# Vision tower with experts: first group's factor products in high and low parts, and a new order of units

## The chip, the cores and the metric

The kernel runs on one core of a Trainium2 chip. The metric is the device time of one execution in microseconds. Before the change the median of three runs is 160.95 us (160.54 to 161.43).

## The reference

32 images of 3 x 96 x 96 become patches of 16 x 16 (36 per image), are projected to 256 features, get a class token (37 tokens per image, 1184 in all) and position terms. Then one block follows: attention of a factored form with running sums instead of softmax, and a layer of 8 experts with two choices per token.

```
h = tok(x)                                        # projection, class token, positions
x1 = layernorm(h)
Q, K = x1 @ Wq.T, x1 @ Wk.T;  Z = cumsum(x1) / counts      # along the 37 tokens
bil = ((Q @ V_b) * cumsum(K @ W_b)) @ U_b.T
tri = ((Q @ V_t) * (Z @ X_t) * cumsum(K @ W_t)) @ U_t.T
h = h + ((bil + alpha * tri) / counts + bias) @ Wo.T
x2 = layernorm(h)
gates = softmax(x2 @ w_router + b_router);  top 2; capacity 185 tokens per expert, in token order
y = weighted sum over the kept choices of (gelu(x2 @ w1[e] + b1[e]) @ w2[e] + b2[e])
out = h + y
```

The order of tokens matters twice: the running sums go along an image, and a token's place with an expert is the count of earlier tokens that chose it.

## The kernel before, in words

Features lie on partitions where products are taken (`h_t`, `xn_t`), tokens on partitions where rows are normalised (`xn`, `h2`). The 1184 tokens are ten tiles of 128, in four groups, GROUPS (L26): A tiles 0 to 2, B_ 3 to 5, C 6 and 7, E 8 and 9 (E has 160 tokens, since the last tile holds 32). In the texts a unit is written zc(A), norm2(C) and so on.

The front part of the kernel is a pipeline over groups, written out by hand in four lists. UNITS (L281) is TensorE's order; each unit is a kind, a group and one of four pairs of PSUM banks (the third number). Before a unit is written, `claim` (L1133) makes TensorE wait until the unit that had this pair before has been read by its last reader. The kinds:
- proj: patches times the projection; B_ and C in high and low parts (SPLIT). On VectorE `proj` adds the position terms into `h_t`.
- norm1: transposes of `h_t`; VectorE takes the statistics (`stats1`, `rstd1`), ScalarE the root (`root1`) and the normalised rows (`norm1`).
- xn_t: transposes of these rows back; ScalarE copies them to `xn_t` (`xn_copy`). For a group in PARTED (L37) ScalarE rounds them to float32r (`xn_high`) and VectorE takes the rest (`xn_low`).
- zc and a: the factor products, `factor_product` (L1121). zc holds the two factors whose results go into running sums, a the third. A group outside PARTED uses two float32 products per factor (one for each half of the features); a group in PARTED uses six of float32r: high x high, low x high, high x low. The factors' parts `m_h` and `m_l` are made on ScalarE (`m_high`) and GpSimd.
- VectorE's `sums` are the scans, GpSimd multiplies the scaled sums into `prod`, VectorE's `prod` multiplies by a. y is the output product, `add_up` adds it to `h_t` giving `h2_t`.
- norm2: transposes of `h2_t` with the router products; ScalarE reads the means (`means2`), sums the squares (`squares2`), takes the root (`root2`), copies the rows kept for the output (`keep2`) and writes the normalised rows (`rows2`) after VectorE's reciprocal and logits (`rstd2`).
- slots and pick: the choices are made in two parts (CHOICES, L30: tiles 0 to 5 and 6 to 9). VectorE's `choose` finds the two experts of each token, slots counts on TensorE who came earlier, VectorE's `place` writes one-hot rows for expert 0, `count` reads all places, and pick multiplies the rows by the one-hots, giving the input of expert 0. Tile 5 of the first part is held back to the second pick (HELD).

BRIDGES (L28) puts products with no use ahead of a unit as filler: four ahead of slots(0), three ahead of pick(0), each two records. They stand behind the unit's `claim`. DVE_ORDER (L291) and ACT_ORDER (L296) are the orders of VectorE and ScalarE, POOL_ORDER that of GpSimd's products. SP's queue stores rows in the order in which rows2 and keep2 stand in ACT_ORDER; GpSimd's gathers for experts 1 and 2 wait for these stores and for the looked-up rows `src_row`.

Then come eight experts: up product, gelu, down product (from expert 1 on in high and low parts, with `hid_hl` for the hidden rows), turned out, weighted and added to the output by indirect DMA.

Of the kernel before, what the change touches and what calls it, by code (L numbers as in the profile page):

```python
# [11 lines left out]
KD = D // 128  # L12
# [15 lines left out]
BRIDGES = {('slots', 0): 4, ('pick', 0): 3}  # L28
# [8 lines left out]
PARTED = (1,)  # L37
INSIDE = KP // 2 - 1
GROUP = max(n for _, n in GROUPS) * TT
EVEN = max(GROUPS[g][1] for g in PARTED) * TT  # L40
# [57 lines left out]
def vit_block(nc, first, patches, const, vectors, attn, w1, w2, b2_rows, xrows, out):  # L98
# [6 lines left out]
    with ExitStack() as ctx:  # L105
# [22 lines left out]
        def spread(per_choice, tiles, n, p=TT):  # L128
# [25 lines left out]
        xn_h, xn_l = (t[:, :, :].rearrange("p k n -> p (k n)")[:, 0:KD * EVEN].rearrange("p (k n) -> p k n", k=KD)  # L154
                      for t in (patch_h, patch_l))
# [12 lines left out]
        hid_hl = sb("hid_hl", [128, KF, 2, SL], f32r)  # L168
        out_t, out_low = held(KF + 2 * KD, KD), held(KF + 3 * KD, KD)
# [61 lines left out]
        def bank(b):  # L231
# [50 lines left out]
                 ("norm1", B_, 2), ("xn_t", A, 0), ("proj", E, 3), ("norm1", C, 1), ("xn_t", B_, 0), ("zc", A, 2),  # L282
                 ("zc", B_, 3), ("a", A, 0), ("a", B_, 1), ("norm1", E, 2), ("xn_t", C, 3), ("y", A, 0), ("zc", C, 3),
                 ("y", B_, 1), ("xn_t", E, 2), ("norm2", A, 0), ("zc", E, 3), ("norm2", B_, 2), ("a", E, 1), ("a", C, 3),
                 ("y", E, 1), ("y", C, 3), ("norm2", E, 0), ("slots", 0, 1), ("norm2", C, 2), ("pick", 0, 3),
                 ("slots", 1, 1), ("pick", 1, 3)]
        PLACE = {(kind, n): u for u, (kind, n) in enumerate(unit[:2] for unit in UNITS if unit[0] != "pick")}
        PICK_SLOT = 3


        DVE_ORDER = [("proj", A), ("uw", 0), ("proj", B_), ("proj", C), ("stats1", B_), ("rstd1", B_), ("proj", E),  # L291
                     ("stats1", C), ("xn_low", B_), ("rstd1", C), ("sums", A), ("sums", B_), ("prod", A), ("stats1", E),
                     ("prod", B_), ("rstd1", E), ("add_up", A), ("sums", C), ("add_up", B_), ("sums", E), ("rstd2", A),
                     ("prod", E), ("prod", C), ("rstd2", B_), ("add_up", E), ("choose", 0), ("add_up", C), ("place", 0),
                     ("count", 0), ("rstd2", E), ("rstd2", C), ("choose", 1), ("below", 0), ("place", 1), ("count", 1)]
        ACT_ORDER = [("mac", 0), ("root1", A), ("norm1", A), ("m_high", 0), ("xn_copy", A), ("root1", B_), ("norm1", B_),  # L296
# [791 lines left out]
        def _(pe):  # L1088
# [32 lines left out]
            def factor_product(dst, n, m, factor):  # L1121

                products = [(factor, xn_t[n % 2])]
                if n in PARTED:
                    products = [(m_h[:, m], xn_h), (m_l[:, m], xn_h), (m_h[:, m], xn_l)]
# [302 lines left out]
```

## Time and profile before

| | us |
|---|---|
| median of three runs | 160.95 |
| lowest and highest | 160.54, 161.43 |
| the profiled execution | 159.94 |
| its span, first to last instruction | 158.1 |
| TensorE, VectorE, ScalarE, GpSimd busy in it | 149.5, 103.4, 82.1, 50.8 |

The profile is of one execution. Its page gives busy time by engine, 40 slices of the span, and the chain of work that ended last. A group of instructions is shown with the line that issued it, the tile that it writes and the ones it reads, and how often. On TensorE a float32 product has two records. Ends of matmuls are modelled and overlap the next start by some 0.17 us, so rates are taken from start to start. In this program's lines, L1129 are the factor products, L1162 and L1236 the transposes, L1250 the output product, L1117 the pick, L1146 the filler, L1299 the first up products of expert 0.

### The profile page before, as it was taken

Reading aid. Unit: us, or ns where it says so; the run is one execution under the profiler, and the core shown is the slowest. Engines: PE = TensorE matmul, PEld = TensorE weight load, DVE = VectorE, ACT = ScalarE, POOL = GpSimd, SP = SyncE. Lnnn points to the kernel's source line nnn. Section 1 sums busy time; section 2 is a strip of 40 time slices with the busy share of each in tenths; the row PEclk is TensorE's granted clock in tenths of the full one; section 3 lists DMA queues with packets and bytes.
Section 4 is the critical chain, followed back from the end, with each engine's and each line's share of the span. In section 5 each row is a group of like instructions: output and inputs, shape, how many; then the busy total and the mean of one; then the engine's idle time right before and its main releaser. Section 6 shows DMA issues by size and latency. Waiting matters only on the chain.

```text
span 158.1 us, 3015 instructions
## 1 busy us (share of the span) xinstructions
PE 149.5 (95%) x1010; PEld 139.4 (88%) x1010; DVE 103.4 (65%) x331; ACT 82.1 (52%) x210; POOL 50.8 (32%) x55
## 2 busy tenths in 40 slices
PE   7999999999999889999999999999999999999950
PEld 7559999978788788899799899999999999999950
DVE  0076874579766988981396859669486795794710
ACT  4215544640528989657055657474582665737100
POOL 6003005007230000004537158085372661604351
PEclk9999999999999999999999999999999999999999
DMA  5999960079002273100489887788868988600421
GB/s 173 420 427 406 405 221 0 0 252 326 8 0 92 100 249 130 51 0 26 106 335 298 269 265 185 266 202 300 280 117 281 264 249 255 139 8 0 52 25 23
DMA packets 17123, 28.48 MB, mean 180 GB/s; under 512 B 1149, under 2 KB 13607, under 8 KB 16857
## 3 DMA queue, kind: packets, MB, share of 16 engines
q1 hardware_dynamic: 14649, 25.49, 47.0%
q0 software_dynamic: 2464, 2.86, 10.3%
q8 instruction: 6, 0.10, 0.3%
q14 instruction: 4, 0.03, 0.1%
HBM read 24.21 MB, written 4.14 MB: 179 GB/s over the span
## 4 chain that ended last, share of the span: by engine, by line
PE 69%; DMA 9%; DVE 8%; issue 4%; ACT 3%; POOL 2%; POOLq 1%; SPq 1%; DVEq 0%; ACTq 0%
PE ps L1287 18%; PE ps L1322 10%; PE ps L1225 7%; PE ps L1207 6%; PE ps L1129 6%; DMA w_even<-w 5%; PE ps L1324 4%; PE ps L1162 3%; DMA out_rows<-out_s,dst_row 3%; PE ps L1141 2%; POOL out_rows L496 2%; PE ps L1167 2%; PE ps L1299 2%; DMA rows_in<-xrows,src_row 2%; PE ps L1250 2%
## 5 line engine op out<-in xcount | busy, mean ns | idle before, releaser
L496 POOL DMA_INDIRECT out_rows<-out_s,dst_row x16 | 23.8, 1485 | 38.6 <-ACT out_s L681 32.2
L657 ACT ACTIVATE first_t<-ps,b_cur 128x186 f32<-128x186 f32 x64 | 23.0, 413 | 23.7 <-PE ps L1287 22.1
L1322 PE MATMUL ps<-hid_hl,split 128*128 128x372 f32 x96 | 29.1, 370 | 0.0
L1324 PE MATMUL ps<-hid_hl,split 128*128 128x186 f32 x96 | 23.8, 248 | 0.0
L1287 PE MATMUL ps<-first_t,patch_t 128*128 128x186 f32 x128 | 21.7, 322 | 0.1
L975 DVE CAST hid_hl<-first_t 128x372 fp32r<-128x372 f32 x28 | 10.7, 383 | 15.8 <-ACT first_t L657 15.8
L1287 PEld LDWEIGHTS ps<-first_t,patch_t 128*128 128x128 f32 x128 | 20.1, 190 | 0.4 <-issue 0.4
L481 POOL DMA_INDIRECT rows_in<-xrows,src_row x14 | 15.6, 1112 | 12.9 <-DVE src_row L943 9.0
L1287 PE MATMUL ps<-first_t,w_even 128*128 128x186 f32 x112 | 18.9, 321 | 0.0
L1324 PEld LDWEIGHTS ps<-hid_hl,split 128*128 128x128 f32 x96 | 18.3, 191 | 0.0
L521 ACT ACTIVATE split<-patch_t 128x512 fp32r<-128x512 f32 (+2 forms) x28 | 13.7, 552 | 8.8 <-DMA patch_t<-patches 5.1
L1322 PEld LDWEIGHTS ps<-hid_hl,split 128*128 128x128 f32 x96 | 18.0, 188 | 0.0
L1287 PEld LDWEIGHTS ps<-first_t,w_even 128*128 128x128 f32 x112 | 17.6, 190 | 0.0
L977 DVE TENSOR_TENSOR hid_hl<-first_t,hid_hl 128x372 fp32r<-128x372 f32 x28 | 15.3, 547 | 1.0
L564 ACT ACTIVATE xn<-ps,nmr,rstd 128x256 f32<-128x256 f32 (+1 forms) x20 | 9.7, 556 | 2.2 <-DVE nmr L740 2.2
L1207 PE MATMUL ps<-split 128*128 128x360 f32 (+1 forms) x72 | 10.6, 305 | 0.0
L983 DVE TENSOR_TENSOR split<-patch_t,split 128x512 fp32r<-128x512 f32 x16 | 10.2, 684 | 0.0
L1207 PEld LDWEIGHTS ps<-split 128*128 128x128 f32 x72 | 10.2, 188 | 0.0
L521 ACT ACTIVATE first_t<-ps 128x186 f32<-128x186 f32 x13 | 4.2, 322 | 10.7 <-PE ps L1324 9.7
L1225 PE MATMUL ps<-first_t 128*128 128x396 f32 x24 | 8.5, 510 | 0.0
L983 DVE TENSOR_TENSOR split<-w_even,split 128x512 fp32r<-128x512 f32 x12 | 7.7, 685 | 0.9 <-ACT split L521 0.9
L1225 PEld LDWEIGHTS ps<-first_t 128*128 128x128 f32 x24 | 4.5, 197 | 3.5 <-DMA first_t<-first 0.7
(175 smaller groups left out, 268.8 us busy)
## 6 DMA issues: line engine op xcount, KB each, us to landing
w_even<-w SPq DMA_DIRECT2D x8, 1024.0 KB, 5.7
patch_t<-w SPq DMA_DIRECT2D x8, 1024.0 KB, 5.3
att<-attn SPq DMA_DIRECT2D x1, 1280.0 KB, 8.5
patch_t<-patches SPq DMA_DIRECT2D x1, 1080.0 KB, 10.7
first_t<-first SPq DMA_DIRECT2D x1, 978.0 KB, 6.1
out_rows<-h SPq DMA_DIRECT2D x2, 384.0 KB, 2.9
xrows<-xn SPq DMA_DIRECT2D x2, 384.0 KB, 2.6
patch_t<-patches SPq DMA_DIRECT2D x1, 756.0 KB, 12.1
```

The lines of the kernel that those rows point to most:

```text
L481: pool.indirect_dma_start(out=rows_in[q][0:SIZES[s], s, :], out_offset=None, in_=xrows[:, :], in_offset=bass.IndirectOffsetOnAxis(ap=src_r ...
L496: pool.indirect_dma_start(out=out[:, :], out_offset=bass.IndirectOffsetOnAxis(ap=dst_row[0:SIZES[s], c:c + 1], axis=0), in_=out_s[q][0:SIZ ...
L521: return act.activation(dst, src, ACT.Copy)
L657: ins = act.activation(hid[:, f, :], bank(pair)[:, (f % 2) * SL:(f % 2 + 1) * SL], ACT.Gelu, bias=b1_cur[q][:, f:f + 1])
L975: dve.tensor_copy(hid_hl[:, f, 0], hid[:, f]).then_inc(hid_high, 1)
L977: dve.tensor_tensor(hid_hl[:, f, 1], hid[:, f], hid_hl[:, f, 0], ALU.subtract).then_inc(hid_split, 1)
L983: dve.tensor_tensor(w2_l[q][:, f], w2_s[q][:, f], w2_h[q][:, f], ALU.subtract).then_inc(w2_split, 1)
L1207: ins = pe.matmul(p[:, d * 512:d * 512 + nb * NP2], w[:, k, d * 128:(d + 1) * 128], x[:, k, 0:patch_width(n)], start=k + m == 0, stop=k == ...
L1225: ins = pe.matmul(p[:, d * 512:d * 512 + nb * NP2], tok_wt[:, k, d * 128:(d + 1) * 128], src[:, k, :], start=k == 0, stop=k == KP - 1)
L1287: ins = pe.matmul(bank(pair)[:, (f % 2) * SL:(f % 2 + 1) * SL], w1_s[q][:, k, f * 128:(f + 1) * 128], buf_t[q][:, k, :], start=k == 0, sto ...
L1322: pe.matmul(dst[:, 0:2 * SL], w2_h[q][:, f, cols], hid_hl[:, f].rearrange("p a s -> p (a s)"), start=f == 0, stop=False)
L1324: ins = pe.matmul(dst[:, 0:SL], w2_l[q][:, f, cols], hid_hl[:, f, 0], start=False, stop=f == KF - 1)
```

## The change

Group A is put into PARTED, so its factor products are taken in high and low parts as B_'s are. Its two parts lie in `hid_hl`, the memory of the experts' hidden rows; B_'s stay in the memory of the patches' parts. Kind a gets its own waits for the group's xn_t copy and, for a group in PARTED, for the factors' low parts, since a may now stand ahead of zc. The four lists are new: norm1(C) ahead of proj(E), a(E) ahead of zc(E), norm2(E) and norm2(C) both ahead of slots(0), add_up(E) ahead of rstd2(B_), add_up(C) ahead of the first choice, rows2(B_) between means2(C) and squares2(C), rows2(C) last on ScalarE, pick on bank pair 2. The filler falls from four products to two ahead of slots(0), and from three to two ahead of pick(0).

```diff
--- before.py
+++ after.py
@@ -25,7 +25,7 @@
 KP = CH * PATCH * PATCH // 128
 GROUPS = [(0, 3), (3, 3), (6, 2), (8, 2)]
 HELD = 1
-BRIDGES = {('slots', 0): 4, ('pick', 0): 3}
+BRIDGES = {('slots', 0): 2, ('pick', 0): 2}
 WARM_UP = 6
 CHOICES = [(0, 6), (6, 4)]
 ENDS = [0] + [min(B, -(-(t0 + n) * TT // T)) for t0, n in GROUPS]
@@ -34,7 +34,7 @@
 FIRST = PATCHES[0][1] * NP2
 PIECES = [(0, 1), (1, 3), (3, KP)]
 SPLIT = (1, 2)
-PARTED = (1,)
+PARTED = (0, 1)
 INSIDE = KP // 2 - 1
 GROUP = max(n for _, n in GROUPS) * TT
 EVEN = max(GROUPS[g][1] for g in PARTED) * TT
@@ -151,8 +151,6 @@
         h2_t = sb("h2_t", [128, KD, N])
 
         xn_t = [sb(f"xn_t{q}", [128, KD, GROUP]) for q in range(2)]
-        xn_h, xn_l = (t[:, :, :].rearrange("p k n -> p (k n)")[:, 0:KD * EVEN].rearrange("p (k n) -> p k n", k=KD)
-                      for t in (patch_h, patch_l))
         same_image = sb("same_image", [128, N])
         z_s = sb("z_s", [128, N])
         z_run, c_run = (first_t[:, :, :].rearrange("p k d -> p (k d)")[:, i * N:(i + 1) * N] for i in range(2))
@@ -166,6 +164,9 @@
 
         hid, buf_t = held(0, KF), [held(KF, KD), held(KF + KD, KD)]
         hid_hl = sb("hid_hl", [128, KF, 2, SL], f32r)
+        flat_parts = hid_hl[:, :, :, :].rearrange("p f a s -> p (f a s)")
+        xn_parts = {0: [wide(flat_parts[:, i * KD * EVEN:(i + 1) * KD * EVEN]) for i in range(2)],
+                    1: [wide(t[:, :, :].rearrange("p k n -> p (k n)")[:, 0:KD * EVEN]) for t in (patch_h, patch_l)]}
         out_t, out_low = held(KF + 2 * KD, KD), held(KF + 3 * KD, KD)
         out_s = [sb(f"out_s{q}", [ST, SLOT_TILES, D]) for q in range(2)]
 
@@ -279,25 +280,27 @@
 
         A, B_, C, E = range(len(GROUPS))
         UNITS = [("proj", A, 0), ("mac", 0, 1), ("uw", 0, 2), ("norm1", A, 0), ("proj", B_, 3), ("proj", C, 1),
-                 ("norm1", B_, 2), ("xn_t", A, 0), ("proj", E, 3), ("norm1", C, 1), ("xn_t", B_, 0), ("zc", A, 2),
-                 ("zc", B_, 3), ("a", A, 0), ("a", B_, 1), ("norm1", E, 2), ("xn_t", C, 3), ("y", A, 0), ("zc", C, 3),
-                 ("y", B_, 1), ("xn_t", E, 2), ("norm2", A, 0), ("zc", E, 3), ("norm2", B_, 2), ("a", E, 1), ("a", C, 3),
-                 ("y", E, 1), ("y", C, 3), ("norm2", E, 0), ("slots", 0, 1), ("norm2", C, 2), ("pick", 0, 3),
-                 ("slots", 1, 1), ("pick", 1, 3)]
+                 ("norm1", B_, 2), ("xn_t", A, 3), ("norm1", C, 0), ("proj", E, 1), ("xn_t", B_, 3), ("zc", A, 2),
+                 ("zc", B_, 1), ("a", A, 0), ("norm1", E, 3), ("a", B_, 2), ("xn_t", C, 1), ("y", A, 0), ("zc", C, 1),
+                 ("norm2", A, 0), ("xn_t", E, 3), ("y", B_, 2), ("a", E, 1), ("zc", E, 3), ("norm2", B_, 2), ("a", C, 3),
+                 ("y", E, 0), ("y", C, 1), ("norm2", E, 3), ("norm2", C, 0), ("slots", 0, 1), ("pick", 0, 2),
+                 ("slots", 1, 1), ("pick", 1, 2)]
         PLACE = {(kind, n): u for u, (kind, n) in enumerate(unit[:2] for unit in UNITS if unit[0] != "pick")}
-        PICK_SLOT = 3
-
-
-        DVE_ORDER = [("proj", A), ("uw", 0), ("proj", B_), ("proj", C), ("stats1", B_), ("rstd1", B_), ("proj", E),
-                     ("stats1", C), ("xn_low", B_), ("rstd1", C), ("sums", A), ("sums", B_), ("prod", A), ("stats1", E),
-                     ("prod", B_), ("rstd1", E), ("add_up", A), ("sums", C), ("add_up", B_), ("sums", E), ("rstd2", A),
-                     ("prod", E), ("prod", C), ("rstd2", B_), ("add_up", E), ("choose", 0), ("add_up", C), ("place", 0),
-                     ("count", 0), ("rstd2", E), ("rstd2", C), ("choose", 1), ("below", 0), ("place", 1), ("count", 1)]
-        ACT_ORDER = [("mac", 0), ("root1", A), ("norm1", A), ("m_high", 0), ("xn_copy", A), ("root1", B_), ("norm1", B_),
-                     ("xn_high", B_), ("root1", C), ("norm1", C), ("xn_copy", C), ("root1", E), ("norm1", E), ("xn_copy", E),
-                     ("means2", A), ("squares2", A), ("keep2", A), ("root2", A), ("means2", B_), ("squares2", B_),
-                     ("root2", B_), ("rows2", A), ("rows2", B_), ("keep2", B_), ("means2", E), ("keep2", E), ("squares2", E),
-                     ("root2", E), ("means2", C), ("squares2", C), ("root2", C), ("rows2", E), ("rows2", C), ("keep2", C)]
+        PICK_SLOT = 2
+
+
+        DVE_ORDER = [("proj", A), ("uw", 0), ("proj", B_), ("proj", C), ("stats1", B_), ("rstd1", B_), ("xn_low", A),
+                     ("stats1", C), ("rstd1", C), ("proj", E), ("xn_low", B_), ("sums", A), ("sums", B_), ("prod", A),
+                     ("stats1", E), ("rstd1", E), ("add_up", A), ("prod", B_), ("sums", C), ("add_up", B_), ("rstd2", A),
+                     ("sums", E), ("prod", E), ("prod", C), ("add_up", E), ("rstd2", B_), ("add_up", C), ("choose", 0),
+                     ("rstd2", E), ("place", 0), ("count", 0), ("rstd2", C), ("choose", 1), ("below", 0), ("place", 1),
+                     ("count", 1)]
+        ACT_ORDER = [("mac", 0), ("root1", A), ("m_high", 0), ("norm1", A), ("xn_high", A), ("root1", B_), ("norm1", B_),
+                     ("root1", C), ("xn_high", B_), ("norm1", C), ("xn_copy", C), ("root1", E), ("norm1", E), ("means2", A),
+                     ("xn_copy", E), ("squares2", A), ("root2", A), ("keep2", A), ("rows2", A), ("means2", B_),
+                     ("squares2", B_), ("root2", B_), ("keep2", B_), ("means2", E), ("squares2", E), ("root2", E),
+                     ("means2", C), ("rows2", B_), ("squares2", C), ("root2", C), ("keep2", E), ("rows2", E), ("keep2", C),
+                     ("rows2", C)]
         POOL_ORDER = (A, B_, C)
         EARLY = [("stats1", A), ("rstd1", A)]
 
@@ -624,7 +627,7 @@
                 elif kind == "xn_high":
                     p = filled(act, "xn_t", n).rearrange("p (k s) -> p k s", k=KD)
                     w = group_width(n)
-                    copy(xn_h[:, :, 0:w], p[:, :, 0:w]).then_inc(xn_high, 1)
+                    copy(xn_parts[n][0][:, :, 0:w], p[:, :, 0:w]).then_inc(xn_high, 1)
                 elif kind == "xn_copy":
                     p = filled(act, "xn_t", n).rearrange("p (k s) -> p k s", k=KD)
                     w = group_width(n)
@@ -889,7 +892,8 @@
                     w = group_width(n)
                     p = filled(dve, "xn_t", n).rearrange("p (k s) -> p k s", k=KD)[:, :, 0:w]
                     dve.wait_ge(xn_high, PARTED.index(n) + 1)
-                    dve.tensor_tensor(xn_l[:, :, 0:w], p, xn_h[:, :, 0:w], ALU.subtract).then_inc(dve_drained, 1)
+                    high, low = xn_parts[n]
+                    dve.tensor_tensor(low[:, :, 0:w], p, high[:, :, 0:w], ALU.subtract).then_inc(dve_drained, 1)
                 elif kind == "sums":
                     running_sums(n)
                 elif kind == "prod":
@@ -1122,7 +1126,8 @@
 
                 products = [(factor, xn_t[n % 2])]
                 if n in PARTED:
-                    products = [(m_h[:, m], xn_h), (m_l[:, m], xn_h), (m_h[:, m], xn_l)]
+                    high, low = xn_parts[n]
+                    products = [(m_h[:, m], high), (m_l[:, m], high), (m_h[:, m], low)]
                 width = EVEN if n in PARTED else group_width(n)
                 for i, (w, x) in enumerate(products):
                     for k in range(KD):
@@ -1242,6 +1247,9 @@
                     factor_product(p[:, 0:512], n, 2, xt_pad)
                     ins = factor_product(p[:, 512:1024], n, 1, m_c)
                 elif kind == "a":
+                    drained(pe, "xn_t", n)
+                    if n in PARTED:
+                        pe.wait_ge(m_split, 3)
                     ins = factor_product(p[:, 0:512], n, 0, m_a)
                 elif kind == "y":
                     c0, c1 = group_cols(n)
```

## Rows read from the trace of the kernel before

**Rows 1.** the page, slices: granted TensorE clock in tenths, 40 equal slices of the span

```profile
PEclk9999999999999999999999999999999999999999
```

**Rows 2.** chain that ended last, in order of time: start us, us, what

```profile
32.48 7.04 PE ps L1129 x30
...
50.19 1.49 ACT xn L555 x6
...
62.16 0.19 PE ps L1262
...
66.16 0.87 PE ps L1299 x4
```

**Rows 3.** timeline of GpSimd, first gather: start us, us, instruction [idle before <-what ended it]

```profile
72.86 1.14 POOL L481 DMA_INDIRECT rows_in<-xrows,src_row  x1 [8.99 <-DVE src_row L943]
```

**Rows 4.** busy us in stretches: PE, PEld, DVE, ACT, POOL; clock, DMA share, GB/s

```profile
44.50:49.90 5.40, 5.40 (x50) 5.36 (x49) 2.88 (x7) 2.99 (x10) 1.30 (x2) 1.00 0.00 0
49.90:55.60 5.70, 5.23 (x37) 4.15 (x36) 5.28 (x38) 5.57 (x18) 0.00 (x0) 1.00 0.41 139
55.60:60.30 4.70, 4.23 (x40) 4.08 (x39) 3.77 (x22) 4.05 (x16) 0.00 (x0) 1.00 0.63 206
```

**Rows 5.** timeline of VectorE, low part of B; reciprocal of B to reciprocal of C

```profile
33.43 0.96 DVE L892 TENSOR_TENSOR split<-ps,split 128x768 fp32r<-128x768 f32 x1 [0.55 <-ACT split L521]
...
52.03 0.18 DVE L731 RECIPROCAL rstd<-std 128x3 f32<-128x3 f32 x1
...
52.73 0.67 DVE L803 SCALAR_TENSOR_TENSOR h_t<-ps,bias_o,h_t 128x160 f32<-128x160 f32 x2
53.32 0.50 DVE L787 MAX8 top<-logit 128x8 f32<-128x8 f32 x6
...
55.55 0.87 DVE L803 SCALAR_TENSOR_TENSOR h_t<-ps,bias_o,h_t 128x256 f32<-128x256 f32 x2
56.34 0.15 DVE L815 SCALAR_TENSOR_TENSOR place<-ps,chosen 128x6 f32<-128x6 f32 x1
...
57.89 0.25 DVE L824 TENSOR_TENSOR by_expert<-is_one,ps 128x96 f32<-128x96 f32 x1
58.06 0.20 DVE L731 RECIPROCAL rstd<-std 128x1 f32<-128x1 f32 x2
...
59.58 0.17 DVE L731 RECIPROCAL rstd<-std 128x2 f32<-128x2 f32 x1 [0.79 <-ACT std L533]
```

**Rows 6.** timeline of TensorE, factor products: start us, us, line op out<-in xcount

```profile
32.32 1.46 PE L1129 MATMUL ps<-xn_t,att 128*128 128x384 f32 x4
33.61 1.45 PE L1129 MATMUL ps<-xn_t,m_c 128*128 128x384 f32 x4
...
49.79 1.65 PE L1129 MATMUL ps<-xn_t,m_a 128*128 128x160 f32 x8
```

**Rows 7.** timeline of ScalarE: rounding copy of B; rows of A and B

```profile
32.52 0.81 ACT L521 ACTIVATE split<-ps 128x768 fp32r<-128x768 f32 x1 [1.03 <-PE ps L1236]
...
51.91 2.82 ACT L564 ACTIVATE xn<-ps,nmr,rstd 128x256 f32<-128x256 f32 x6
```

**Rows 8.** timeline of TensorE: warm-up, bridge ahead of pick, pick of the first choice

```profile
1.01 2.93 PE L1141 MATMUL ps<-mean_mat 128*128 128x128 f32 x12 [1.01 <-POOL mean_mat L441]
...
57.80 0.91 PE L1146 MATMUL ps<-mean_mat 128*128 128x128 f32 x6
...
58.55 3.32 PE L1117 MATMUL ps<-onehot,xn 128*128 128x186 f32 x20
61.71 0.30 PE L1260 MATMUL ps<-chosen,ones 128*128 128x32 bf16 x6
```

## The prediction

> **What bounds the kernel now.** The granted clock and the row of slices come first: the clock is full in all 40 slices [rows 1], so nothing below is a matter of clock. Then the chain of work that ended last, in order of time. From 66.16 us on it is the experts: TensorE work with fixed partners, started by the first product of expert 0 [rows 2]. Everything there hangs on what the front part hands over, since the gathers wait for the looked-up rows (GpSimd idle 8.99 us until src_row [rows 3]) and the later weight loads wait for the gathers and the experts' products. So the question is when the first expert product starts; what it gains is carried to the end one for one, unless a free-running transfer ends later, and I find none.
>
> Back from 66.16 the chain changes its engine. Up to 49.95 it is TensorE without a gap: the 30 records of factor products take 7.04 us [rows 2], and in 44.50 to 49.90 TensorE is busy 5.40 of 5.40 us while VectorE has 2.88 [rows 4]. From 49.95 it is ScalarE (squares of group B, 1.49 us [rows 2]) and then VectorE: in 49.90 to 55.60 VectorE is busy 5.28 of 5.70 us [rows 4]. VectorE is idle only once after that, 0.79 us ahead of the reciprocal of group C at 59.58 [rows 5], because the transpose norm2(C) waited for add_up(C), which stands behind the first choice. So there are three regions: TensorE bound to 49.95, VectorE bound to 58.8, a wait on a round trip at 59.58 and from there a fixed tail (choice 1, slots, one-hot rows, marks) to 66.16. The reader is to see that time saved on TensorE before 49.95 counts only if ScalarE and VectorE start the B group earlier, and that in the second region it is VectorE's list that counts.
>
> **Part 1, factor products of A by high and low parts.** A full float32 product of 384 columns takes 33.61 - 32.32 = 1.29 us [rows 6]. The 30 records of 7.04 us hold three of these (A) and three split ones (B), so a split product takes (7.04 - 3 x 1.29) / 3 = 1.06 us [rows 2, 6]. Three products of A save 3 x 0.23 = 0.69 us of TensorE. The bounds for A are these two rates: 0 and 0.69; I take 0.69, because shapes and types are those of B. It costs one rounding copy on ScalarE in place of a plain one (both 768 columns; B's takes 0.81 us [rows 7]), and 0.96 us of VectorE for xn_low(A) [rows 5]. That stands at about 29.9 to 30.9 us, where VectorE otherwise waits for proj(E); stats1(C) behind it comes no later than before, because norm1(C) is now transposed before proj(E). It is covered. If that cover were gone it would push xn_high(B), which starts at 32.52 [rows 7] with about 0.4 us to spare. The two parts of xn_t(A) lie in memory of the experts' hidden rows, idle until expert 1. m_high goes ahead of norm1(A) on ScalarE, so norm1(A) ends near 25.7 instead of 24.7, two microseconds before its transpose; GpSimd's m_low ends near 26, needed at 32.3. Both cost nothing. The w1 and w2 loads of expert 1 on SP's queue wait for proj(E), now second: 0.4 us later, with their use some 45 us away. The bound for these moved waits is 0 to 0.1 us.
>
> **Part 2, the order up to the end of norm2(B).** zc(A) still starts at 32.3. zc(B) may start when xn_low(B) is done: 33.43 + 0.96 + 0.15 us to reach TensorE = 34.5 [rows 5], and zc(A) now ends at 34.44, so 0.1 us of the 0.46 us saved there is lost again. After that I went through the new list of TensorE step by step with the durations of this trace, checking each against its bank's reader. Sums, prod and add_up of A, B and C arrive in time (add_up(A) near 42.4 for norm2(A) at 42.7; add_up(B) near 47.6 for norm2(B) at 48.0). a(E) now stands ahead of norm2(B), 0.59 us (eight records of a(E) and a(C) take 1.65 us, 1.48 without the tail of the last, of which 160 of 416 columns and the weight loads make 0.6 [rows 6]). The sum to the end of norm2(B) is -0.69 + 0.1 + 0.6 = 0.0. So ScalarE starts on B at about 50.05 as before, and the reciprocal of B stays at 52.03 to 52.14. The saved product time does not move the chain here; it buys earlier products of E and C. Before, y(E) and y(C) came late enough that add_up(E) ran behind rstd2(B); now a(C), y(E), y(C) end near 52.6, and add_up(E) runs from 51.5 to 52.1, in the gap in which VectorE waits for the root of B. The new wait of a on its xn_t copy holds only a(E), whose copy ends at 45.6 against 46.3.
>
> **Part 3, VectorE from the reciprocal of B.** Before [rows 5]: rstd2(B) 52.03 to 52.73, add_up(E) to 53.32, choice 0 to 55.55, add_up(C) to 56.34, place and six one-hot rows to 57.89, count and rstd2(E) to 58.79, then 0.79 idle. After: rstd2(B) 0.70, add_up(C) 0.79, choice 0 2.23, rstd2(E) 0.65 (0.73 from its start to its last end), place 1.55, count 0.17: 6.09 us from 52.14, that is 58.24. add_up(E) 0.59 has left the list, the idle 0.79 is gone if the root of C is there in time, and the start is 0.11 later: 59.58 - 58.24 = 1.34 us at most. The root of C: add_up(C) ends at 53.71, norm2(C) follows at 53.86 and ends at 55.26. ScalarE has the root of E until 55.4, then the means of C 0.2, rows2(B), which is now put ahead of the squares, 1.37 (six tiles take 2.82 [rows 7]), then two tiles of squares 1.03 (three take 1.49 [rows 2]) and 0.35 for the root and its way to VectorE (51.68 to 52.03 [rows 2, 5]): 58.35. So rstd2(C) starts at 58.35 instead of 59.58, 1.23 us earlier. Three waits meet within 0.1 us of each other here (root of B against add_up(E), means of C against norm2(C), root of C against count), and none has slack.
>
> **Part 4, the slots of the second choice.** From rstd2(C) to the slots' first product it was 62.16 - 59.58 = 2.58 us [rows 2, 5], which would give 60.93. But pick(0) stands ahead on TensorE. It now lies on bank pair 2, whose last reader is rows2(B), ending at 57.07; pick(0), slots(1) and pick(1) are queued behind that wait, and VectorE's place(1) waits for slots(1). With 0.15 us for the way, two bridge products (six records of three products took 58.55 - 57.80 = 0.75 us, so 0.5 [rows 8]) and the five tiles (58.55 to 61.71, 3.16 us [rows 8]) pick(0) is out at 60.88, the six products of L1260 at 61.13. So slots(1) starts its own product at 61.13, not 60.93: 1.03 us earlier than 62.16. The shortened bridge ahead of slots(0) costs and gives nothing, since slots(0) waits for the choice anyway (idle 0.3 us instead of filler); that of pick(0) lies behind the wait, so each product cut is worth 0.25 us. The rest of the tail (one-hot rows, marks, pick(1)) is unchanged and moves with it. rows2(C), now last on ScalarE, ends at 61.2 and pick(1) needs it when the first one-hot row of C is there at 61.8. SP's stores of E and C rows go out near 61.5 as before, and GpSimd wants them at 71.8 (72.86 before [rows 3]). Nothing there is late.
>
> **Sum.** Expert 0 starts at 66.16 - 1.03 = 65.1 us. The profiled execution has a span of 158.1 in 159.94 us; after, 157.1 in 158.9. The median of the runs shown is 160.95, 1.0 above the profiled one, and by it the forecast is 160.95 - 1.05 = 159.9 us. Bounds from the unknown: the best is choice-bound, -1.25 (159.7); with A's products at the rate of B gained or not, and each of the three tied waits 0.1 late, -0.6 (160.3).
>
> **Rivals.** (a) *The new wait on rows2(B) is the bound and takes more.* Everything queued behind pick(0) moves one for one with rows2(B). If ScalarE reaches it 0.5 us later than I say (norm2(C) or root E late, or the copies keep2 running longer), the gain is 0.2 to 0.7 us: 160.25 to 160.75, read as no change. For it: ScalarE is busy 4.05 of 4.70 us in 55.60 to 60.30 already [rows 4], and no slack stands ahead of it. Against: the same steps in the same shapes stood in the trace with spaces of 0.02 us. (b) *The gain is given back behind 66 us,* or the edit does not speed A up and the ties use up the rest: within 0.2 us of 160.95. Against: no transfer there runs free of the chain. (c) *TensorE's clock falls.* Slower than before: by my list TensorE is idle some 1.7 us of 50.7 to 57.8 (y(C) 0.2, norm2(C) 0.3, slots(0) 0.4, pick(0) 0.8), where before it is idle 0.47 of 5.70 and 0.47 of 4.70 [rows 4], and the cut bridges are the filler. Price: the first twelve records take 2.93 us, 0.23 each, against 0.125 for the same records in a bridge [rows 8], though the clock row reads full in both; at that rate pick(0) takes 5.8 instead of 3.2 us and pick(1) as much again: +2.7 to +5.4, less 1.05, so 162.6 to 165.3. It decides from the point at which the granted clock falls below 1.00 in 52 to 60 us. Against it: before, the clock held through those gaps, each under 0.5 us; the longest new gap is 0.9 us.
>
> The Trainium skill says on this, in "TensorE: Matmul & The Clock Gate", section "What's actually happening", that "the default state is throttled, and activity releases the throttle"; by that rule filler cut from a thin stretch speaks against this change, and the time would be that of rival (c). The trace of before shows no fall at all, so it bears the rule out nowhere but in the slow first records, and I give it little.
>
> **How the numbers follow.** Under 0.5% (0.80 us) a measurement of this kernel can't tell a difference from none. Forecast (gain 0.8 to 1.35): 0.63. Rival (a): 0.20. Rival (b): 0.08. Rival (c): 0.06. Slower by another way, such as a wait of the new order that I put at nothing: 0.03. So faster 0.64, same 0.27, slower 0.09. The likeliest time is 159.9; the range leaves out rival (c) and the outer part of (b) and has 0.4 us added on the lower side for the scatter of the runs (160.54 to 161.43): 159.2 to 161.0.
>
> **What would show it.** In the profile after: L1129 holds records of split parts for A and no 384-column float32 ones; the three products of A fall from 3.87 to 3.2 us; means2(B) starts near 50.0 as before; add_up(E) stands ahead of rstd2(B), add_up(C) near 52.8; rstd2(C) near 58.4; pick(0) starts at 57.7 behind rows2(B); slots(1) near 61.1; the first L1299 near 65.1; granted clock 1.00. I am wrong if norm2(B) ends later than 50.3, if pick(0) starts after 58.2, or if the distance from L1299 to the end differs from 158.1 - 66.16 = 91.9 us.

## The result, and the profile after

The changed kernel's median of six executions is 161.44 us (158.65 to 162.63), against 161.1 (160.54 to 161.43) for the kernel before. This number can't be understood without one fact: in four of the six TensorE's mean granted clock is 0.975 to 0.982 and the time 161.35 to 162.63, in the other two it is 0.993 and 0.994 and the time 158.65 and 158.68. By the two in which the clock held, the ratio to the kernel before is 0.985, interval 0.981 to 0.989. So both things that the prediction weighed took place: the change is faster where the clock holds, by more than forecast, and in about half of its executions (9 of 18 with the next run) the clock falls and takes it all back. Below, "the clock falls" means such an execution: all those counted as fallen have a mean granted clock of 0.983 or less, all those in which it held 0.987 or more.

The profiled execution (158.65 us, span 156.7) is one in which the clock holds until TensorE is done. The page's row of the granted clock, to be held against [rows 1] (its last slice lies behind the last product):

```profile
PEclk9999999999999999999999999999999999999997
```

The chain in order of time, the rows that answer [rows 2] (start us, us, what):

```profile
3.94 8.54 PE ps L1230 x24
...
32.63 5.41 PE ps L1134 x30
...
38.48 1.06 PE ps L1134 x6
...
57.01 0.91 ACT xn L558 x4
```

All six products of A and B are now split: 36 records in 5.41 + 1.06 = 6.47 us instead of 30 in 7.04 [rows 2]; norm1(E) stands between the two rows. The squares of C now stand in the chain at 57.0. The busy time of the same stretches as [rows 4] (columns as there):

```profile
44.50:49.90 5.40, 5.40 (x42) 4.87 (x41) 3.22 (x11) 4.41 (x13) 0.89 (x2) 1.00 0.15 50
49.90:55.60 5.70, 5.49 (x40) 4.56 (x41) 4.95 (x34) 4.46 (x20) 0.00 (x0) 1.00 0.49 164
55.60:60.30 4.70, 3.83 (x32) 3.58 (x31) 4.45 (x34) 4.67 (x15) 0.00 (x0) 1.00 0.35 118
```

TensorE is busy 3.83 of 4.70 us in the last of them, before 4.23. VectorE, the rows that answer [rows 5]:

```profile
51.66 0.68 DVE L806 SCALAR_TENSOR_TENSOR h_t<-ps,bias_o,h_t 128x160 f32<-128x160 f32 x2 [0.15 <-PE ps L1258]
52.25 0.16 DVE L734 RECIPROCAL rstd<-std 128x3 f32<-128x3 f32 x1
...
52.94 0.87 DVE L806 SCALAR_TENSOR_TENSOR h_t<-ps,bias_o,h_t 128x256 f32<-128x256 f32 x2
53.73 0.50 DVE L790 MAX8 top<-logit 128x8 f32<-128x8 f32 x6
...
58.32 0.16 DVE L734 RECIPROCAL rstd<-std 128x2 f32<-128x2 f32 x1
```

add_up(E) is ahead of the reciprocal of B, add_up(C) ahead of the first choice, and the reciprocal of C is at 58.32 with no idle ahead of it (before 59.58 after 0.79 idle). TensorE, the rows that answer [rows 8]:

```profile
55.19 0.69 PE L1151 MATMUL ps<-mean_mat 128*128 128x128 f32 x4
56.18 0.18 PE L1270 MATMUL ps<-chosen,neg_prefix 128*128 128x48 bf16 x1 [0.30 <-DVE chosen L799]
56.20 0.29 PE L1272 MATMUL ps<-chosen,ones 128*128 128x48 bf16 x6
57.06 0.71 PE L1151 MATMUL ps<-mean_mat 128*128 128x128 f32 x4 [0.57 <-ACT xn L567]
57.61 3.32 PE L1121 MATMUL ps<-onehot,xn 128*128 128x186 f32 x20
60.77 0.30 PE L1268 MATMUL ps<-chosen,ones 128*128 128x32 bf16 x6
60.92 0.18 PE L1270 MATMUL ps<-chosen,neg_prefix 128*128 128x32 bf16 x1
```

L1151 is the filler (L1146 before), L1121 the pick (L1117), L1270 the first product of slots. The pick waits for rows2(B) and for two filler products, as forecast, and slots(1) starts at 60.92 instead of 62.16. The first expert product comes at 64.91 (before 66.16), and the first gather, 72.86 in [rows 3], at 71.61.

For the comparisons below each trace is cut at fixed places, worked out from its timeline: the first product behind the first projection ("start"), the end of norm2(B), the first expert product, the turning of expert 0's output, the last product, the end. Each column is the time from one place to the next. The traces of e3 and e11 are of executions in which the clock fell.

```
us                          start  to norm2(B)  to first   to turning  to last   tail  span
                                   end          expert     of exp. 0   product
before                      12.17  37.76        16.23      24.37       61.93     5.64  158.1
before, 2nd trace (e6)      12.84  37.76        16.22      24.37       61.90     5.91  159.0
after                       12.31  37.70        14.90      24.24       61.92     5.63  156.7
after, 2nd trace (e1)       12.28  37.70        14.89      24.29       61.93     6.01  157.1
e2  filler 4 and 3          13.08  37.72        15.12      24.42       61.93     5.63  157.9
e3  before, filler 2 and 2  12.90  37.74        18.88      24.15       61.90     5.73  161.3
e4  no filler               12.30  37.69        14.89      24.56       61.93     5.73  157.1
e5  filler first            13.01  37.69        14.89      24.51       61.91     5.69  157.7
e7  before, A split         12.29  37.63        16.22      24.53       61.90     5.73  158.3
e8  new order, A float32    12.26  38.33        15.12      24.08       62.23     5.98  158.0
e10 filler 4 and 2          13.07  37.69        14.90      24.45       61.94     5.65  157.7
e11 filler 2 and 3          12.71  37.71        18.06      24.96       61.90     5.76  161.1
e12 filler first            12.24  37.69        14.89      24.32       61.91     5.75  156.8
```

The columns "to norm2(B) end" and "to first expert" carry the change: -0.06 and -1.33 us, -1.39 in sum. The start column differs by up to 0.9 us between executions, by 0.7 and 0.8 between two of the same kernel (before and e6; e12 and e5), and has nothing to do with the change.

### The profile page after: what moved, and what is told of

It reads as the page before. It is cut to its first block, busy times and chain, and to the rows that moved or that the text cites. A ratio compares the mean times of both kernels' runs of the same rounds, so it can differ in the third digit from the quotient of the medians.

```text
span 156.7 us, 3021 instructions
## 1 busy us (share of the span) xinstructions
PE 148.3 (95%) x1010; PEld 139.7 (89%) x1010; DVE 104.2 (66%) x332; ACT 82.2 (52%) x210; POOL 50.9 (32%) x55
## 4 chain that ended last, share of the span: by engine, by line
PE 67%; issue 12%; DMA 7%; ACT 6%; POOL 2%; DVE 2%; POOLq 1%; SPq 1%; DVEq 0%; ACTq 0%
PE ps L1295 16%; PE ps L1330 10%; PE ps L1230 7%; PE ps L1134 7%; PE ps L1212 7%; DMA w_even<-w 5%; PE ps L1332 4%; PE ps L1258 3%; DMA out_rows<-out_s,dst_row 3%; PE ps L1167 3%; ACT xn L567 2%; PE ps L1146 2%; POOL out_rows L499 2%; PE ps L1172 2%; PE ps L1340 2%
```

## The experiments

**Does the clock fall again, and does filler hold it?** The kernel unaltered, twelve executions more:

> The changed kernel, unaltered, on the chip of the next three. Theory 1 (clock): its executions fall into two kinds, one near 158.7 us with a mean granted clock of 0.99, one near 161.5 us with 0.98, because in some of them TensorE's clock falls in the thin stretch between 55 and 58 us. Theory 2 (chip): the longer kind belongs to the chip of the first measurement and the kernel before shows it here as often. Expected by 1: both kinds again, the kernel before with one kind only, at 160.5 to 161.4.

The clock fell in five of twelve (161.04 to 162.86 us, mean granted clock 0.974 to 0.981), in seven it held (158.49 to 159.37). Together with the first six that is 9 of 18. The kernel before, in 29 executions between them, has none below 0.988. Theory 2 falls. No execution of the changed kernel in which the clock fell was traced; the two traces of a fall, below, are of the old order (e3) and of the new order with one more product ahead of the pick (e11).

```diff
-BRIDGES = {('slots', 0): 2, ('pick', 0): 2}
+BRIDGES = {('slots', 0): 4, ('pick', 0): 3}
```

> The changed kernel with the filler of before (four products ahead of slots(0), three ahead of pick(0)). Theory 1 (the cut filler lets the clock fall): no execution of the longer kind; the product more ahead of pick(0) stands behind its wait and costs 0.25 us, so about 158.9 us. Rival (the thin stretch is thin by the order, whatever the filler: the wait of pick(0) on rows2(B) comes first and the filler behind it): the longer kind is as frequent as in the changed kernel.

No fall in six. The median is 159.5 us, ratio 0.989 (0.985 to 0.993). In the table the first expert product is 0.22 us later than in the changed kernel: the one more product behind the pick's wait, as costed. The median is 0.6 us above the 158.9 expected; that is taken up below, with the starts.

```diff
 # the kernel before
-BRIDGES = {('slots', 0): 4, ('pick', 0): 3}
+BRIDGES = {('slots', 0): 2, ('pick', 0): 2}
```

> The kernel before with the filler cut to two and two, nothing else. Theory 1: the clock falls in some executions, and those are 2 to 3 us longer than the kernel before. Rival (order): slots(0) and norm2(C) leave gaps of 0.5 us or less here, the clock stays and the time is that of the kernel before or up to 0.25 us less (pick(0) earlier by one product, though slots(1) waits for the choice anyway).

In five of thirteen executions the clock fell (163.1 to 163.8 us), in eight it held (ratio 0.996, interval 0.993 to 0.999). The kernel before has no fall in the 29 executions measured beside them. So the cut of the filler alone does it, in the old order too, and the rival falls. Its profile is of an execution with the fall. The page's clock row, then busy time by stretch (columns as in [rows 4]):

```profile
PEclk9999999999999955999999999999999999999997
```

```profile
56.00:57.00 1.00, 0.43 (x9) 0.25 (x7) 0.96 (x4) 1.00 (x6) 0.00 (x0) 1.00 0.80 258
57.00:58.00 1.00, 0.73 (x4) 0.76 (x5) 0.96 (x6) 0.97 (x6) 0.00 (x0) 0.53 1.01 349
58.00:63.00 5.00, 5.00 (x21) 5.00 (x22) 2.92 (x24) 3.28 (x11) 0.00 (x0) 0.50 0.26 83
63.00:64.00 1.00, 1.00 (x5) 1.00 (x5) 0.93 (x11) 0.98 (x3) 0.00 (x0) 0.56 0.52 164
64.00:65.00 1.00, 1.00 (x8) 1.00 (x7) 0.16 (x2) 0.99 (x2) 0.00 (x0) 1.00 0.92 305
```

The third figure from the right (0.50) is the granted clock: from just after 57 to just before 64 us it is one half, the lower of its two levels (1.2 instead of 2.4 GHz), though TensorE is busy without a gap from 57.3 on. Its timeline has what it did before and what it paid:

```profile
55.41 0.71 PE L1146 MATMUL ps<-mean_mat 128*128 128x128 f32 x4
56.49 0.18 PE L1262 MATMUL ps<-chosen,neg_prefix 128*128 128x48 bf16 x1 [0.37 <-DVE chosen L796]
56.51 0.29 PE L1264 MATMUL ps<-chosen,ones 128*128 128x48 bf16 x6
57.27 0.66 PE L1162 MATMUL ps<-cst,h_t 128*128 128x128 f32 x2 [0.47 <-DVE h_t L803]
57.73 0.86 PE L1167 MATMUL ps<-wr_c,h_t 128*128 128x9 f32 x4
58.44 0.67 PE L1162 MATMUL ps<-cst,h_t 128*128 128x128 f32 x2
58.90 0.86 PE L1167 MATMUL ps<-wr_c,h_t 128*128 128x9 f32 x4
59.62 1.20 PE L1146 MATMUL ps<-mean_mat 128*128 128x128 f32 x4
60.61 4.93 PE L1117 MATMUL ps<-onehot,xn 128*128 128x186 f32 x20
```

The clock falls inside the gap ahead of 57.27; that gap is 0.47 us, and none in the three microseconds ahead of it is longer. The pick takes 4.93 instead of 3.32 us [rows 8], and the first expert product comes 18.88 us after norm2(B) instead of 16.22: 2.66 us for one fall.

```diff
-BRIDGES = {('slots', 0): 2, ('pick', 0): 2}
+BRIDGES = {}
```

> The changed kernel without any filler. Theory 1: nearly every execution is of the longer kind, so that the profile shows where the clock falls (I expect in 55 to 60 us) and what it costs: pick(0), 3.2 us at the full clock, takes up to 6. Rival: as often as in the changed kernel; then the executions that keep the clock gain 0.4 us, since pick(0) starts two products (0.5 us) sooner and the choice (0.2 us) bounds slots(1).

Eight of ten executions have a mean clock of 0.967 to 0.983 (160.7 to 162.0 us), two hold it (158.9). That is the direction of theory 1, though 8 of 10 against the 9 of 18 of the changed kernel can be chance. Two parts of the expectation missed: the profile is of an execution that held its clock, and that one gained nothing. Its pick started 0.35 us sooner (57.25), held by the first one-hot row, and slots(1) was at 60.88 all the same: there the second choice, not the pick, is the bound. The ratio of 0.997 that belongs to this kernel mixes both kinds of execution and is no measure of the work. And its two waits are longer than any in e3, with the clock held:

```profile
56.17 0.18 PE L1270 MATMUL ps<-chosen,neg_prefix 128*128 128x48 bf16 x1 [0.85 <-DVE chosen L799]
57.25 3.39 PE L1121 MATMUL ps<-onehot,xn 128*128 128x186 f32 x20 [0.76 <-DVE onehot L820]
```

So the length of a gap doesn't settle what a single execution does; the filler shifts the share of executions that fall.

**Which of the two fillers?**

```diff
-BRIDGES = {('slots', 0): 2, ('pick', 0): 2}
+BRIDGES = {('slots', 0): 4, ('pick', 0): 2}
```

> The changed kernel with four filler products ahead of slots(0) and two ahead of pick(0). If the clock is held by the filler ahead of slots(0), which fills 0.5 us of a wait that is there anyway, no execution with the lower clock and no time lost: first expert product 14.9 us after norm2(B). If it is the one ahead of pick(0): some with the lower clock.

No fall in nine, and no time lost: 14.90 us from norm2(B) to the first expert product, to the hundredth that of the changed kernel. Median 159.5 us, ratio 0.992 (0.990 to 0.995).

```diff
-BRIDGES = {('slots', 0): 2, ('pick', 0): 2}
+BRIDGES = {('slots', 0): 2, ('pick', 0): 3}
```

> The changed kernel with two filler products ahead of slots(0) and three ahead of pick(0). If the filler ahead of slots(0) holds the clock: some executions with the lower clock, about as in the changed kernel (9 of 18), and the others 0.25 us longer. If the one ahead of pick(0) holds it: none.

Two falls in seven (161.4 and 162.9 us), and the profile is of one of them:

```profile
57.48 1.65 PE L1151 MATMUL ps<-mean_mat 128*128 128x128 f32 x6 [0.55 <-ACT xn L567]
58.91 5.59 PE L1121 MATMUL ps<-onehot,xn 128*128 128x186 f32 x20
```

The filler of the pick runs at half rate already. Cut into tenths of a microsecond, the trace has the granted clock at 1.00 up to 56.7 and at 0.50 from there, while slots(0) is running and before the wait of 0.55 us; the gaps ahead of it are 0.18 and 0.30 us. So this filler comes too late to hold the clock. The price here is 18.06 - 15.12 (e2, with the same three products ahead of the pick) = 2.9 us. It is the filler ahead of slots(0) that holds the clock: with four products there, no fall in 38 executions (e2, e5, e8, e10, e12); with two, 16 in 38 (the change twice, e3, e11); with none, 8 in 10. This count leaves out e9, below, in which the same four products stand behind a wait of 2.4 us and the clock fell in all four executions. That a third product ahead of the pick does nothing is less sure: 2 of 7 against 9 of 18 shows no effect, and couldn't show a small one.

**Filler in the wait instead of behind it.** Four products ahead of slots(0), and three that stand ahead of the pick's wait:

```diff
-BRIDGES = {('slots', 0): 2, ('pick', 0): 2}
+BRIDGES = {('slots', 0): 4}
+AHEAD = 3
...
+                if (kind, n) == ("pick", 0):
+                    bridge(AHEAD, slot("slots", 0)[:, 512:640])
                 claim(u)
```

> The changed kernel with four filler products ahead of slots(0), and three ahead of pick(0) that stand before its wait on rows2(B) instead of behind it, written to the idle bank beside slots(0). Theory 1 (cut and misplaced filler lets the clock fall): it fills gaps that are waits anyway, so no execution with a lower clock, and every one at the time of the changed kernel's undisturbed ones (158.9 us on the chip before) or 0.1 less. Rival (the rows2(B) wait and the order thin the stretch too much for any such filler): the lower clock stays in some executions.

> Once more the changed kernel with four filler products ahead of slots(0) and three ahead of pick(0) that stand before its wait. If the filler holds the clock, again no execution with the lower clock (12 of 12 with the first time), a median of 159.2 to 159.5 and a ratio near 0.99; if six executions were luck, at the rate of the changed kernel about three of six.

No fall in thirteen executions of two measurements, medians 159.41 and 159.68 us, ratios 0.991 (0.987 to 0.994) and 0.993 (0.991 to 0.996). The mean of the 13 is 159.4, that of the changed kernel's 18 is 160.3, that of the kernel before, in the 36 executions measured beside them, 160.9. It beats both, against the changed kernel by never falling. It isn't shown to be better than e10, which never fell either (159.50 us, ratio 0.992, beside 159.68 and 0.993 of e12). From the trace of e5:

```profile
57.06 0.91 PE L1152 MATMUL ps<-mean_mat 128*128 128x128 f32 x6
57.96 3.39 PE L1122 MATMUL ps<-onehot,xn 128*128 128x186 f32 x20
61.19 0.30 PE L1271 MATMUL ps<-chosen,ones 128*128 128x32 bf16 x6
61.59 0.19 PE L1273 MATMUL ps<-chosen,neg_prefix 128*128 128x32 bf16 x1
```

Between L1271 and L1273 TensorE now waits for the second choice; the pick has some 0.2 us to spare (0.40 from L1271 to L1273, 0.15 from L1268 to L1270 in the changed kernel) and the filler costs nothing.

**Why is the gain 1.4 us in traces and over 2 in medians of the executions that held the clock?**

> The kernel before, unaltered, for a second trace. The comparison of medians gives the change 2.0 us, the traces 1.4. Theory A (the first trace of before was a lucky one: its inputs landed early): this span is near 159.1, and the microsecond more lies ahead of 16 us, in the loads. Theory B (something inside the front or the experts varies): the microsecond lies between 32 and 66 us or behind it.

The second trace of before has a span of 159.0. Of the 0.9 us more, 0.67 lie ahead of 12.84 us and 0.27 behind the last product; the columns between agree within 0.03 us. So Theory A has the place for most of it, but it isn't the loads: TensorE starts this work at 3.94 and 3.93 us, and it is the earlier trace that still waits for an input there (0.51 us at 5.41), the later one for none. The first projection's 24 records take 8.39 us in the first trace and 9.07 in the second, and in e10 (chain rows of before, of e6 and of e10):

```profile
3.94 8.39 PE ps L1225 x24
```

```profile
3.93 9.07 PE ps L1225 x24
```

```profile
3.94 9.30 PE ps L1230 x24
```

TensorE's weight loads of e10 at that place show why:

```profile
3.94 0.50 PEld L1230 LDWEIGHTS ps<-first_t 128*128 128x128 f32 x2 [0.30 <-DMA first_t<-first]
4.76 0.34 PEld L1230 LDWEIGHTS ps<-first_t 128*128 128x128 f32 x1 [0.32 <-issue]
5.42 0.34 PEld L1230 LDWEIGHTS ps<-first_t 128*128 128x128 f32 x1 [0.32 <-issue]
6.08 1.86 PEld L1230 LDWEIGHTS ps<-first_t 128*128 128x128 f32 x6 [0.32 <-issue]
```

The loads are 0.66 us apart until 6.08, then 0.33: the engine still runs at half rate for the first two microseconds of this unit, in other executions for less, though the clock row reads full. When the rate rises differs from one execution to the next.

That can explain the medians. Where the clock is held by filler, starts of both kinds are counted: e10 does the changed kernel's work in the changed kernel's time (14.90), and its nine executions have a median of 159.5. The changed kernel's nine that held the clock have 158.74. The changed kernel seems to hold its clock mostly after an early start: the five traces with thin filler or none are three that held (starts 12.28 to 12.31) and two that fell (12.71 and 12.90), while with full filler clocks held at starts up to 13.08. Five traces are few, so this is consistent, not proven. There is more for it on record. On one chip, the seven held executions of e1 have a median of 158.77 and the six of e5, at the same work in the front part, 159.41. And the eight of e3 that held have 160.4 against 161.0 for the kernel before, though by the trace of before the pick was not the bound there and a shorter filler saves nothing. If so, the ratio of 0.985 counts the lucky starts of one kernel against all starts of the other, and the ratio of the work is rather that of e5, e10 and e12: 0.991 to 0.993, some 1.1 to 1.5 us.

**What do the products bring, and what the order?**

(Shortened; the memory of the parts and the waits of kind a are as in the change.)

```diff
 # the lists and the filler of before
-PARTED = (1,)
+PARTED = (0, 1)
...
-("rstd1", B_), ("proj", E),
+("rstd1", B_), ("xn_low", A), ("proj", E),
...
-("xn_copy", A)
+("xn_high", A)
```

> The lists and the filler of before, with group A's factor products in high and low parts (xn_high and xn_low of A put in, nothing else). Theory (prediction's part 1 and 2): TensorE is the bound to the end of norm2(B), so 0.69 less 0.1 us come off there and everything behind moves with it: 0.6 us off, ratio 0.996. Rival (VectorE's xn_low(A) and proj(E) come into the way, or reciprocal of A at 49.6 holds): no change.

Ratio 0.999 (0.996 to 1.003), and in the trace norm2(B) ends 0.13 us earlier, not 0.6. zc(B) starts at 35.03, behind a wait (TensorE, then VectorE's xn_low(B) in this kernel, then in the changed one):

```profile
35.03 0.59 PE L1132 MATMUL ps<-split,m_h 128*128 128x384 f32 x2 [0.30 <-DVE split L894]
```

```profile
33.97 0.96 DVE L894 TENSOR_TENSOR split<-ps,split 128x768 fp32r<-128x768 f32 x1 [0.96 <-ACT split L522]
```

```profile
33.58 0.96 DVE L896 TENSOR_TENSOR split<-ps,split 128x768 fp32r<-128x768 f32 x1 [0.47 <-ACT split L524]
```

All that zc(A) saves is lost there (35.03 against 33.61 + 1.29 = 34.90 before [rows 6], with a start 0.12 us later), since zc(B) can't start before xn_low(B) is done. Why xn_low(B) starts 0.50 us after the end of ScalarE's copy here, and 0.10 us in the changed kernel, no row tells; that stays open.

```diff
-PARTED = (0, 1)
+PARTED = (1,)
...
-("rstd1", B_), ("xn_low", A),
+("rstd1", B_),
...
-("xn_high", A)
+("xn_copy", A)
-BRIDGES = {('slots', 0): 2, ('pick', 0): 2}
+BRIDGES = {('slots', 0): 4, ('pick', 0): 3}
```

> The lists of after with the filler of before (4 and 3), but group A's factor products in plain float32. Theory: norm2(B) ends 0.6 to 0.7 us later and everything behind it, so 0.6 us above the changed kernel with the same filler (159.5): 160.1. Rival (slack in the VectorE part takes it up): 159.5.

160.2 us against 159.5 of e2, which has the same filler; norm2(B) ends 0.61 us later (38.33 against 37.72), and the column behind it is the same, 15.12. So the products are worth 0.6 us in the new order and 0.1 in the old one, and the new order 16.22 - 15.12 = 1.1 us behind norm2(B), less the 0.57 us that it puts ahead of it. With the 0.22 of the filler product cut from the pick this gives 1.10 - 0.57 + 0.61 + 0.22 = 1.36 of the 1.39 us.

```diff
-("norm2", C, 0), ("slots", 0, 1)
+("slots", 0, 1), ("norm2", C, 0)
...
-("rstd2", B_), ("add_up", C), ("choose", 0)
+("rstd2", B_), ("choose", 0), ("add_up", C)
-BRIDGES = {('slots', 0): 2, ('pick', 0): 2}
+BRIDGES = {('slots', 0): 4, ('pick', 0): 3}
```

> The lists of after with the filler of before (4 and 3), but add_up(C) behind the first choice and norm2(C) behind slots(0), as they stood before. Theory: norm2(C) starts about 2 us later and VectorE again waits for the root of C ahead of rstd2(C), so the first expert product comes 0.5 to 0.8 us later than in the changed kernel with that filler: 15.7 us after the end of norm2(B) instead of 15.12. Rival (ScalarE's rows2(B), which no longer stands ahead of the squares when they become ready, gives it back): 15.1 to 15.2.

166.3 us, ratio 1.034 (1.031 to 1.038), with the clock at 0.960 to 0.975 in all four executions. Both theories missed, because neither looked at the banks: slots(0) lies on the pair of y(C), so it can't start before add_up(C) has read it, filler included, and add_up(C) now stands behind the first choice.

```profile
57.12 1.57 PE L1151 MATMUL ps<-mean_mat 128*128 128x128 f32 x8 [2.44 <-DVE h_t L806]
```

```profile
56.00:57.00 1.00, 0.00 (x0) 0.00 (x0) 0.97 (x5) 0.48 (x2) 0.00 (x0) 1.00 0.00 0
57.00:58.00 1.00, 0.88 (x6) 0.88 (x7) 0.68 (x7) 0.00 (x0) 0.00 (x0) 0.85 0.00 0
58.00:67.00 9.00, 7.36 (x38) 7.20 (x37) 4.33 (x30) 5.67 (x17) 0.00 (x0) 0.50 0.24 80
67.00:68.00 1.00, 1.00 (x5) 1.00 (x4) 0.00 (x0) 1.00 (x1) 0.00 (x0) 0.53 0.67 217
```

TensorE idles 2.44 us, the clock falls while the filler behind the wait is already running (0.85 in 57 to 58), and stays at half until just before 68 us, through a second wait of 1.64 us. This doesn't price add_up(C)'s place; it shows that the new bank pairs and the place of add_up(C) are one decision, and what a gap costs.

## Why the prediction was wrong

**The sign and the chance of the clock's fall.** Rival (c) got 6 in 100 and came in 9 of 18 executions, in the stretch named (52 to 60 us; 57.0 in e3, 56.7 in e11) and at the lower end of the price named (2.7 to 5.4 us; 2.7 in e3, 2.9 in e11, and 161.53 - 158.74 = 2.8 between the medians of the changed kernel's two kinds). The step that failed stands in part 4: the shortened bridge ahead of slots(0) "costs and gives nothing, since slots(0) waits for the choice anyway". As time on the path that is right (e10 has two products more there and loses nothing). As cover it is the only filler that matters: 0 of 38 against 16 of 38. And the argument against the rival, that the clock held through the gaps of before, was drawn from a trace with the filler in place; it told nothing of a kernel without it. The idle time that it reckoned with was even too high: 1.7 us in 50.7 to 57.8, where the changed kernel's trace has 1.08 in 50.8 to 57.8, hardly more than the 0.94 of before in [rows 4]. By the sentence of the Trainium skill quoted there ("TensorE: Matmul & The Clock Gate", "What's actually happening"), activity releases the throttle: the trace of e3 agrees, with the clock back at 1.00 just before 64 us, after TensorE had been busy without a gap from 57.3 on. That two products more ahead of slots(0) hold the clock is what the counts show.

**The size of the gain.** Forecast -1.05, and -1.39 between the traces, so the mechanism was right here and a few terms were off. To the end of norm2(B) I had +0.1 against measured -0.06: a(E) costs 0.54 (46.42 to 46.96), not 0.6, and the wait of zc(B) is as forecast. Behind it I had 15.08 and it is 14.90: the six products of L1268 take 0.15 us (60.77 to 60.92), not 0.25, and the pick follows its wait a little sooner. Part 4 put the pick's path 0.2 us behind that of the choice (61.13 against 60.93); the two tie. From the end of norm2(B) to slots(1) it is 10.91 us in the changed kernel and 10.89 in e4 and e5, whose pick has time to spare. The rest of the chain came as listed: norm2(B) at 50.01 (50.05 forecast), reciprocal of B 52.25, of C 58.32 (58.35), pick 57.61 (57.72), slots(1) 60.92 (61.13), first expert product 64.91 (65.1). Behind it 0.13 us more come off up to the turning of expert 0's output, within the spread of that column (24.08 to 24.96), and are no part of the change.

**The range.** 159.2 to 161.0 holds neither kind of execution: the nine of the changed kernel that fell have a median of 161.53, the nine that held 158.74, and the 161.44 measured first is that of four falls in six. Another draw of the same kernel, e1, had a median of 159.26, inside the range, and that would have been luck. The range left out a case that is half of all executions, and took the start as given: the profiled execution of before had an early one, which is most of why it lay 1.0 us under the median. The medians of e2, e5, e10 and e12, in which the clock always held, are 159.4 to 159.7 and lie in it.

**Right:** that the products buy nothing at norm2(B) by themselves but time for E and C, that the idle of 0.79 us ahead of the reciprocal of C goes, that the pick has a new wait on rows2(B) and each product behind it costs 0.25 us (0.22 in e2), that the tail behind the experts' start doesn't change. I had not said that the old order gives the products nothing: by my part 2 it should have given them 0.6, and e7 says 0.1.

## What to carry to other kernels

Filler on TensorE is to be judged by what clock it holds, not by the path: ask how each thin stretch looks without it, and put it ahead of the wait, into a bank that is free, where it costs nothing and comes in time. Count the executions by their granted clock before comparing medians; a kernel whose clock falls in half of them has no single time, and those that held it may be the ones with the lucky start (here consistent with the traces, not proven). A saving of one part and a new order have to be tried each alone: here the products were worth 0.1 us in the old lists, where a wait whose cause is open takes the rest, and 0.6 in the new ones.

## What the runs showed of the hardware that I had not expected

The granted clock fell to one half after stretches in which TensorE was never idle for more than 0.5 us at a time (e3) and for more than 0.3 us (e11), and stayed there for nearly 7 us, most of them without a gap. In e9 it stayed there for 10 us. Yet it held through gaps of 0.85 and 0.76 us in a trace without filler (e4). Two filler products, 0.5 us of work, decide between no fall in 38 executions and 16 in 38. The start of a kernel varies by 0.9 us (8.39 to 9.30 us for the same 24 records) with the moment at which the rate of the first products doubles, and the clock row of the profile reads full there. In most traces the clock row falls behind the last product too (0.7 in the last slice), so that a mean of 0.99 says nothing against a kernel, while 0.98 does.
